# Two stages of an audio tower reordered: dispatch scores and the two-way scan

## The reference

```python
def _L1_attn_ref(x, ...):              # the two-way stage
    xn = layer_norm(x, ln_g, ln_b)
    xg, z = split(xn @ Wi + bi)
    f = simple_ssm(conv1d_same(xg, Wf_conv, bf_conv), af, bf, cf, df)
    bb = flip(simple_ssm(conv1d_same(flip(xg), Wb_conv, bb_conv), ab, bb, cb, db))
    zg = silu(z)
    return (f * zg + bb * zg) @ Wo + bo + x

# soft mixture; dispatch makes the logits, both softmaxes and the slots' inputs
    phi_n = phi * rsqrt(sum(square(phi), axis=0) + EPS_NORM)
    # logits of 374 tokens against 64 * 16 = 1024 slots;
    # softmax over tokens gives dispatch weights, softmax over slots combine weights;
    # slot inputs = dispatch weights^T @ tokens, then layer norm, 64 experts, combine
```

## Time and profile before

| what | value |
|---|---|
| median of 3 runs | 2442.38 us (2439.57 to 2445.49) |
| the profiled execution, its own time | 2446.13 us |
| its span in the trace | 2444.3 us |
| two-way stage in the trace | about 1698 to 1875 us |
| dispatch in the trace | about 1878 to 2201 us |
| mean granted clock of TensorE | 0.956 of full |

### The profile page before, as it was taken

The page is one execution under the profiler, slowest core; times in us unless marked ns, Lnnn a source line. Parts: engine busy times, 40 slices in busy tenths (PEclk is TensorE's granted clock), DMA queues, the critical chain, the costliest instruction groups (busy, mean ns, idle before and its releaser), DMA issues. The chain is left out here.

```text
span 2444.3 us, 45740 instructions
## 1 busy us (share of the span) xinstructions
PE 2208.8 (90%) x16643; PEld 2025.3 (83%) x16643; DVE 1361.5 (56%) x3616; ACT 1143.7 (47%) x2203; POOL 861.7 (35%) x760
## 2 busy tenths in 40 slices
PE   2999999999999999999999877976997888968988
PEld 1999999999999999999999876975554666658988
DVE  4676667667667667676666642413674555532222
ACT  1655655565555555555555532222442555532320
POOL 4444555555554554555655521102220000000000
PEclk9999999999999999999999987988998898988999
DMA  5700000000000000000000212492000011009966
GB/s 164 227 4 4 4 4 4 7 6 4 9 5 5 9 4 5 9 4 5 9 4 2 64 36 83 146 255 78 18 15 0 39 43 46 39 38 303 332 209 223
DMA packets 101337, 150.65 MB, mean 62 GB/s; under 512 B 14693, under 2 KB 79119, under 8 KB 100365
## 3 DMA queue, kind: packets, MB, share of 16 engines
q1 hardware_dynamic: 77580, 118.36, 15.4%
q10 hardware_dynamic: 17984, 20.30, 2.5%
q0 software_dynamic: 5568, 9.27, 1.3%
HBM read 102.32 MB, written 45.50 MB: 60 GB/s over the span
## 5 line engine op out<-in xcount | busy, mean ns | idle before, releaser
L290 PE MATMUL banks<-t_wt,t_l 128*128 128x128 f32 x8508 | 1045.9, 277 | 4.1 <-ACT t_l L367 2.9
L290 PEld LDWEIGHTS banks<-t_wt,t_l 128*128 128x128 f32 x8508 | 1015.5, 193 | 19.5 <-ACT t_l L367 4.1
L466 POOL TENSOR_TENSOR t_rstd<-t_var,t_minus_half 128x4 f32<-128x4 f32 (+1 forms) x379 | 367.0, 968 | 639.0 <-DVE t_var L395 637.6
L349 ACT ACTIVATE t_sq<-banks 128x512 f32<-128x512 f32 (+1 forms) x379 | 216.2, 570 | 523.1 <-PE banks L290 521.3
L403 DVE TENSOR_TENSOR t_yn<-banks,t_rstd 128x512 f32<-128x512 f32 (+1 forms) x379 | 249.0, 657 | 366.2 <-POOL t_rstd L466 364.4
L383 ACT ACTIVATE t_l<-banks,t_cols 128x512 f32<-128x512 f32 x376 | 286.8, 778 | 78.9 <-PE banks L339 76.2
L472 POOL TENSOR_TENSOR t_zrstd<-t_zvar,t_minus_half 128x8 f32<-128x8 f32 x188 | 307.6, 1637 | 25.4 <-DVE t_zvar L430 25.4
L392 DVE TENSOR_REDUCE t_ss<-t_sq 128x4 f32<-128x512 f32 (+1 forms) x379 | 244.5, 645 | 88.3 <-ACT t_sq L349 82.7
L367 ACT ACTIVATE t_l<-banks,t_cols 128x512 f32<-128x512 f32 (+1 forms) x381 | 285.1, 748 | 12.5 <-PE banks L299 7.7
L299 PE MATMUL banks<-t_ident,t_yn 128*128 128x128 f32 x1426 | 220.0, 274 | 13.0 <-DVE t_yn L403 11.7
L299 PEld LDWEIGHTS banks<-t_ident,t_yn 128*128 128x128 f32 x1426 | 173.3, 142 | 27.1 <-DVE t_yn L403 14.8
(11 more groups left out here) (324 smaller groups left out, 3332.5 us busy)
## 6 DMA issues: line engine op xcount, KB each, us to landing
t_w<-in_w SPq DMA_DIRECT2D x64, 480.0 KB
t_w<-in_w SPq DMA_DIRECT2D x27, 576.0 KB, 5.7
ect<-t_ECT SPq DMA_DIRECT2D x16, 750.0 KB, 3.2
t_l<-in_w1a SPq DMA_DIRECT2D x27, 384.0 KB, 4.3
sorted_by_expert<-t_h SPq DMA_DIRECT2D x4, 2400.0 KB, 11.0
routed_by_expert<-t_h SPq DMA_DIRECT2D x4, 2400.0 KB, 17.5
t_ectb<-ect ACTq DMA_DIRECT2D x5, 1500.0 KB, 7.9
t_w1x<-in_w1x SPq DMA_DIRECT2D x64, 97.5 KB
```

The source lines that it names most:

```text
L290: mm = pe.matmul(psY[bank][:, t * C:(t + 1) * C], src[:, at:at + P], T["wt"][:, 3 * (layer - 1) + k, :], start=(k == 0), stop=(k == 2))
L349: act.activation(T["sq"][:, par, 0:n], psY[bank][:, 0:n], ACT.Square).then_inc(S["squared"], 1)
L466: pool.tensor_tensor(T["rstd"][:, par, 0:n], T["var"][:, par, 0:n], T["minus_half"][:, 0:n], ALU.pow)\
```

## The change

In the two-way stage the transposes leave `inputs`: `turn(b + 1)` stands ahead of `conv(b, 2)`, and ACT's reads of them stand ahead of bu and du of m = 2. DVE runs `norm(b + 2)` ahead of batch b's scans and adds the output of batch b - 1 after batch b's two additions. The buffer u has three places instead of two, and both places of xh are used. The banks are dealt anew: the outputs get two banks of their own, and the third convolution shares the first one's. In dispatch the three tiles' logits stand in steps 3, 4 and 5 instead of 3 to 6, the turned logits have one bank instead of two, and the turned slot inputs get that second bank instead of sharing pE.

```diff
-    pA, pB, pX, pC, pO = ps[0], ps[1], [ps[2], ps[3]], [ps[4], ps[5], ps[6]], [ps[7], ps[1]]
+    pA, pB, pX, pC, pO = ps[0], ps[1], [ps[2], ps[3]], [ps[4], ps[5], ps[4]], [ps[6], ps[7]]
...
+            def turn(b):
+                pe.wait_ge(S["xh_ready"], b + 1)
+                turn_tiles(pe, T, xh, b, pA, pB).then_inc(S["xh_turned"], 1)
+
             def inputs(b):
-                pe.wait_ge(S["xh_ready"], b + 1)
-                if b >= 2:
-                    pe.wait_ge(S["two_out"], b - 1)
-                turn_tiles(pe, T, xh, 0, pA, pB).then_inc(S["xh_turned"], 1)
...
-                if b >= 1:
-                    pe.wait_ge(S["conv_read"], 6 * (b - 1) + 2 * (m + 1))
+                if m == 2:
+                    pe.wait_ge(S["conv_read"], 6 * b + 2)
+                elif b >= 1:
+                    pe.wait_ge(S["conv_read"], 6 * b - 2 * m)
...
+            turn(0)
+            for b in range(B):
                 inputs(b)
                 conv(b, 0)
                 conv(b, 1)
-                outputs(b - 1)
+                if b >= 1:
+                    outputs(b - 1)
+                if b + 1 < B:
+                    turn(b + 1)
                 conv(b, 2)
...
                 for m in range(3):
+                    if m == 2 and b + 1 < B:
+                        read_turned(b + 1)
...
             for b in range(B):
-                link = Link(dve, S["two_link"], 10, b)
+                if b + 2 < B:
+                    norm(b + 2)
+                link = Link(dve, S["two_link"], 9, b)
...
-                if b + 2 < B:
-                    norm(b + 2)
-                dve.wait_ge(S["two_done"], b + 1)
...
+                if b >= 1:
+                    add_out(b - 1)
+            add_out(B - 1)
...
-    LOGITS_AT, TILE_AT = {3: (0, 1), 4: (2,), 5: (3,), 6: (4, 5)}, {4: 0, 6: 1, 7: 2}
+    LOGITS_AT, TILE_AT = {3: (0, 1), 4: (2, 3), 5: (4, 5)}, {4: 0, 5: 1, 6: 2}
...
-    pT, pE, pC = [ps[4], ps[5]], ps[6], ps[7]
+    pT, pH, pE, pC = ps[4], ps[5], ps[6], ps[7]
...
-                if k >= 2:
-                    pe.wait_ge(S["edt_ready"], k - 1)
+                if k >= 1:
+                    pe.wait_ge(S["edt_ready"], k)
...
-                if pairs_before(at) >= 1:
-                    pe.wait_ge(S["ht_read"], 2 * pairs_before(at))
...
-                pe.wait_ge(S["ed_read"], chunks)
```

More of the change, by code:

```diff
@@ L1673, in _, with read_turned @@
             act.wait_ge(S["pads_zero"], 1)
-            for b in range(B):
+            def read_turned(b):
                 act.wait_ge(S["xh_turned"], b + 1)
@@ L1681, in _ @@
                                scale=T["lncol"][:, 1:2]).then_inc(S["n_ready"], 1)
+            read_turned(0)
+            for b in range(B):
                 if b >= 1:
@@ L1730, in norm, with add_out @@
                 norm_stats(dve, T, S, link, 2 * b, lambda t: htile(T, b, t), D)
-                at = lambda t: a[0:TOK, b % 2, t, :]
+                at = lambda t: a[0:TOK, b % 3, t, :]
                 link(norm_apply(dve, T, lambda t: htile(T, b, t), at))
                 norm_stats(dve, T, S, link, 2 * b + 1, at, D)
-                if b >= 1:
-                    dve.wait_ge(S["xh_turned"], b)
-                norm_apply(dve, T, at, lambda t: xh[0:TOK, 0, t, :]).then_inc(S["xh_ready"], 1)
+                if b >= 2:
+                    dve.wait_ge(S["xh_turned"], b - 1)
+                norm_apply(dve, T, at, lambda t: xh[0:TOK, b % 2, t, :]).then_inc(S["xh_ready"], 1)
+            def add_out(b):
+                dve.wait_ge(S["two_done"], b + 1)
+                for t in range(TPB):
+                    n = min(TOK, LEN - t * TOK)
+                    ins = dve.tensor_tensor(htile(T, b, t)[0:n], htile(T, b, t)[0:n],
+                                            pO[t // 2][0:n, (t % 2) * D:(t % 2 + 1) * D], ALU.add)
+                ins.then_inc(S["two_out"], 1)
             dve.wait_ge(S["sig"], 1)
@@ L1772, in _ @@
                 hb = T["h"][0:TOK, TPB * b:TPB * (b + 1), :]
-                link(dve.tensor_tensor(hb, hb, a[0:TOK, b % 2, :, :], ALU.add))
+                link(dve.tensor_tensor(hb, hb, a[0:TOK, b % 3, :, :], ALU.add))
                 link(dve.tensor_tensor(hb, hb, view(T["rows"][0:TOK, 2, :], [[0, TPB], [1, D]]), ALU.add))
-                if b + 2 < B:
-                    norm(b + 2)
-                dve.wait_ge(S["two_done"], b + 1)
[L1778 to L1783, removed]
+                if b >= 1:
+                    add_out(b - 1)
+            add_out(B - 1)
 def dispatch(nc, T, S, io):
@@ L1887, in slot_inputs, with slot_inputs_turned @@
                 mm.then_inc(S["xs_done"], 1)
-            def slot_inputs_turned(k, chunks):
+            def slot_inputs_turned(k):
                 p = k % PAIRS_B
@@ L1911, in _ @@
                 if k >= 2:
-                    slot_weights_turned(k - 2, k)
+                    slot_weights_turned(k - 2)
                 if k < STEPS:
@@ L1921, in _ @@
                 if pair_at(k) is not None:
-                    slot_inputs_turned(pair_at(k), k - 1)
+                    slot_inputs_turned(pair_at(k))
             for p in (2, 3):
@@ L1925, in _ @@
             for k in range(pairs_before(STEPS + 2), PAIRS_B * B):
-                slot_inputs_turned(k, STEPS)
+                slot_inputs_turned(k)
         @block.scalar
@@ L1952, in copy_slot_inputs @@
                     act.activation(view(T[name][:, :], [[P, 2 * P // SLOT], [1, SLOT]], 2 * p * (P // SLOT) * P + b * SLOT),
-                                   pE[0:r, at:at + 2 * P].rearrange("d (n s) -> d n s", s=SLOT), ACT.Copy)\
+                                   pH[0:r, at:at + 2 * P].rearrange("d (n s) -> d n s", s=SLOT), ACT.Copy)\
                         .then_inc(S["ht_read"], 1)
@@ L1975, in _ @@
                         act.wait_ge(S["ed_turned"], k - 2)
-                    act.activation(EDT[:, k % 3, 0:LEN], pT[k % 2][:, 0:LEN], ACT.Exp, bias=T["ltm"][:, k % 2:k % 2 + 1],
+                    act.activation(EDT[:, k % 3, 0:LEN], pT[:, 0:LEN], ACT.Exp, bias=T["ltm"][:, k % 2:k % 2 + 1],
                                    accum_out=T["zd"][:, k:k + 1]).then_inc(S["edt_ready"], 1)
@@ L2452, in s2 @@
                     sb(name, shape, dt, two)
-                s2("u", [TOK, 2, TPB, D])
+                s2("u", [TOK, 3, TPB, D])
                 s2("xh", [TOK, 2, TPB, D])
```

10 lines of the change are left out of this document (5 added, 5 removed).

## The result

The changed kernel takes 2408.84 us, the median of 4 runs (2408.14 to 2409.43); the kernel before takes 2442.14 us on the same chip, also 4 runs (2439.57 to 2445.49). The ratio is 0.9863, with a 95% interval from 0.9846 to 0.988. The range's bound of 2410 is inside the interval (2404.5 to 2412.8), but the forecast's own middle, 2420.5, is not.

A forecast was written before the change was run, and what follows sets the result against it. PE, the busiest engine but with gaps and below full clock, was taken to bound both stages; 6.5 us (two-way) plus 15.4 (dispatch) gave 21.9, from 2442.4 to 2420.5 us, range 2410 to 2432.

The forecast's parts named there:

- The two-way stage: Late start of 8.2 us, then rounds of 17.5 us instead of 19.34, last outputs waiting 2.6 us more: gain 6.5 us.
- Dispatch's term: Dispatch gains 15.4 us: six batches at 1.9 us (11.4) plus 4.0 us in the last batch.
- The step that failed: Dispatch, middle batches: 0.5 us taken off the 2.4 us gain for the clock falling at step 7's gaps, leaving 1.9.
- The term for the last batch's four steps: Dispatch, last batch: four steps save 0.95 us each (3.8), plus 0.2 at the first slot inputs; 4.0 us, between 2 and 6.
- the walk along the end of a batch: Dispatch, from fifth step: logits end after 8.82 us, next batch's first step 6.09 later, second 1.83 later; 2.4 us gained.
- 2.11 + 0.27: Dispatch, per batch at unchanged clock: logits end 2.11 us earlier, the two steps after them take 7.92 us instead of 8.19.
- (1): Dispatch keeps little: longer round trip or later ACT queue, a batch gains 0.5 us instead of 1.9; 2429 us, chance 0.16.
- (2): Two-way stage gains nothing: rounds cost 18.4 us and the 8.2 us late start eats the rest; 2427 us, chance 0.11.
- (3): Slower: dispatch's clock falls at step 7's gaps and stays down through the slot products; 2469 us, chance 0.06.
- (4): No difference: the stages' gains are handed back before the experts start; chance 0.05 with all near it.
- its last rival: Dispatch: by the skill's rule alone, the single bank with one more short gap a batch would speak for the lower bound.
- The named signs: Expected trace: y(0) near 1743, two-way rounds 17.5 us, batches 34.4 us apart, 16 us in last batch, L's wait gone or short.

The follow-up runs named there:

- e5: Changed kernel with POOL's gathers issued one batch earlier (batches 0 and 1 at the start): 2408.49 us, two-way stage 159.3 us.
- e6: e5 with the output addition of batch 6 moved, in the last batch, ahead of the third scans: 2405.1 us, two-way stage 156.4 us.
- e7: Changed kernel with 14 extra unused transposes on PE in step 7, ahead of the slot inputs: 2409.03 us, dispatch 300.4 us.
- e8: e2 with the same 14 unused transposes behind step 7's slot inputs in the old dispatch: 2425.82 us, dispatch 319.1 us.
- e3: e2 with the logits in steps 3, 4 and 5, banks dealt as before: 2432.08 us, dispatch 324.3 us.
- e2: New two-way stage with the dispatch of the kernel before: 2432.75 us, ratio 0.9966.
- e4: Changed kernel with the logits back in steps 3 to 6, new banks kept: 2418.45 us, dispatch 310.8 us.
- e1: New dispatch with the two-way stage of the kernel before: 2420.47 us, ratio 0.9913.
- e9: e7 with ACT's copy to H ahead of its reads of the tile in steps 6 and 7: 2412.54 us (one run).
- e11: e6 with the 14 extra transposes of e7 and the copy order of e9: 2401.22 us, ratio 0.9842.

## Why the prediction fell short

**The two-way stage was right step by step.** y(0) came 8.1 us late, measured from the stage's start (forecast 8.2), behind a wait of 6.21 us for batch 2's gather; e5 takes that wait away and brings y(0) back to 27.3 us. Rounds took 17.2 us up to y(5) (forecast 17.5). y(7) came 10.3 us earlier (forecast 9.1; the shorter rounds are where the difference comes from), and the last outputs waited 8.78 us (forecast 8.9), which e6 shortened by the 2.7 that the addition costs. Gain 7.6, forecast 6.5.

**Dispatch's term was mis-sized: 15.4 forecast, 23.6 measured.** Its parts, again from transposes of q to transposes of q:

| part of dispatch | before | after | gain | forecast |
|---|---|---|---|---|
| up to batch 0's transposes (starts 1879.0, 1866.3) | 25.7 | 24.9 | 0.9 | 0 |
| round of batch 0 | 35.1 | 35.2 | 0.0 | 0 |
| five rounds of 36.34 and 33.54 | 181.7 | 167.7 | 14.0 | 9.5 |
| last round, to the last batch's fourth step | 35.6 | 33.8 | 1.8 | 1.9 |
| from there to the last slot products | 20.3 | 15.0 | 5.3 | 4.0 |
| from there to the experts | 29.3 | 27.6 | 1.8 | 0 |

**The step that failed** is the one that reads "The changed order has gaps there too, of about 0.8 and 1.9 us in step 7. With the slot products now closer behind them, I take off 0.5 and use 1.9 us a batch." The gaps were there as named (0.57 and 1.79 us), and the clock fell behind them in four of the five rounds, but it cost less: the slow clock cost 0.79 us a round in place of 1.63. I had let the cost grow by 0.5 where it shrank by 0.84. That is 1.3 us a round, against which the gain at full clock was 1.96 instead of the 2.4 that I had worked out, and (1.3 - 0.4) x 5 = 4.5 us make up the difference of the third row. Why the cost of the clock shrank stays open; that it did, the rows show.

The last row is the clock as well: the last 48 slot products have the same shape and took 8.10 us after, at 1.00, and 9.78 before, at 0.83:

```profile
2142.88 8.10 PE L1895 MATMUL banks<-t_q,t_ED 125*128 125x192 f32 x48 [0.71 <-DVE t_ED L2075]
```

It comes with the banks: 8.1 us in all nine profiles with the new banks, 9.7 to 10.9 in the four with the old.

The term for the last batch's four steps was 1.3 us too small, in two places. The last four steps gave 4.5 us (11.33 to 6.80) where 3.8 was forecast: a step came to 1.7 us and not to the round trip of 1.85. The part ahead of them gave 0.75 (8.94 to 8.19) where 0.2 was forecast; the first slot inputs no longer wait 1.38 us for the shared bank. From one execution to another the piece varies: 15.0 to 16.0 us in the nine profiles with the new banks, and 20.3 or 22.4 in the four with the old.

The first row's 0.9 us is no gain of the order. The piece took 24.9 to 26.8 us in the nine profiles with the new banks and 23.6 to 25.7 in the four with the old, longer at the lower clock in each; at a like clock the new order is 1 us or more longer (26.8 at 0.69 against 25.7 at 0.70). The prediction had 0.6 of loss there. The kernel before was profiled in the longer kind and the changed kernel in a shorter one, which is luck.

**At full clock the walk along the end of a batch holds.** In e7 the fifth step is at 2027.85, the row behind the last logits at 2036.67, the next batch's first step at 2042.84 and its second at 2044.68; from its timeline, the wait behind the fill and the second step:

```profile
2042.29 0.30 PE L1907 MATMUL banks<-t_ident,t_xs 128*128 128x128 f32 x1 [0.30 <-ACT t_H L1965]
...
2044.68 0.54 PE L1866 MATMUL banks<-t_ident,t_L 125*128 125x125 f32 x3 [0.24 <-ACT t_EDT L1989]
```

That is 8.82, 6.17 and 1.84 us; the forecast had 8.82, 6.09 and 1.83. In e8, the old order at full clock, they are 10.92, 5.02 and 2.35, where the earlier trace rows have 10.93, 5.01 and 3.18:

```profile
2046.33 1.66 PE L1938 MATMUL banks<-t_ident,t_L 125*128 125x125 f32 x14
2048.18 0.54 PE L1866 MATMUL banks<-t_ident,t_L 125*128 125x125 f32 x3 [0.19 <-ACT t_L L1958]
...
2050.53 0.49 PE L1866 MATMUL banks<-t_ident,t_L 125*128 125x125 f32 x3
```

So the one wrong row in the forecast's sum was before's last piece: the 3.18 us from the first to the second step in the earlier trace rows held 0.83 us of slow clock (2.35 without it). I had counted it as order. (The first row is the fill.) Behind the second step another 0.5 us is gained up to the next transposes, which the forecast left out. Together 2.10 - 1.15 + 0.51 + 0.51 = 1.97 us, the 1.96 of the rounds.

**The split into scores and banks failed too.** "2.11 + 0.27" gave nearly all of the gain to the early scores. Alone they bring 1.0 us of dispatch, no more than noise, and at full clock their round is longer than the old one (35.34 against 34.71). The first share can only be had if ACT's later queue does not hold PE through a shared bank. The last batch's gain belongs to the banks alone, as forecast: from batch 7's transposes to the experts e3 takes 88.1 us and e2 87.2, e4 76.9 and after 76.4.

**The rivals.** (1) and (2) had too little gain; a batch gained 2.8, and the two-way rounds were 17.2. (3), the slower one, named the right lever, the clock at step 7's gaps, and turned out the other way round. (4) fell: every microsecond of the stages reached the experts. The Trainium skill (TensorE: Matmul & The Clock Gate, "A second HAM failure mode: psum-queue depth-cycling") says that short idles between groups, as a kernel cycles through banks, make the clock swing and cost throughput. That agrees with the unequal rounds here, which e7 and e8 make equal by filling the idle. What the prediction drew from it, that one bank fewer for the turned logits would make it worse, does not agree with the rows: the clock of dispatch rose from 0.87 to 0.91. The prediction calls this its last rival, but the list gives it no time and no chance of its own. Here the measurement decides, and the number of banks alone does not tell the clock.

**The named signs.** Of those that the prediction listed, the wait for nB, y(0), the rounds of the two-way stage, the last outputs and the wait for the exponential and for H in step 7 came as described. Batches were 33.5 us apart instead of 34.4, and 15.0 us passed in the last batch instead of 16. In the list of PE's waits for the five rounds after, none has a wait for L, which was 8.4 us before:

```profile
PE banks L1907 <- ACT t_H L1961: 9.0, 5, 1.8
PE banks L1866 <- ACT t_EDT L1985: 3.1, 6, 0.6
PE banks L1895 <- DVE t_ED L2075: 1.9, 4, 0.5
```

## What to carry to other kernels

When rows of one order are taken as durations for another, read the clock beside each: a piece of 3.18 us at the lower level was 2.35 us of order and 0.83 us of clock, and a forecast made from it counts the clock twice or with the wrong sign. Moving work earlier on one engine gained 1.0 us alone, which is within the noise, giving each of two chains a bank of its own gained 14.5, and both 21.2: look first for the bank, buffer or queue that two chains share, since it decides whether an earlier start is kept. Where an unchanged part varies by more than the effect, compare the lengths of the changed stages between events, in more than one execution where the code allows it, and ask the whole time only at the end.

## What the runs showed of the hardware

The granted clock fell behind gaps of 1.7 and 1.8 us in a stretch in which PE was otherwise busy: it was 0.86 to 0.95 in most rounds of dispatch, but not in all of them: behind the same gap of 1.8 us and with the same instructions, 8 of the 20 full rounds of after, e1, e5 and e6 kept 1.00. Fourteen more transposes in the gap, 1.66 us of them in e8, kept it at 1.00 in all 25 full rounds of the five kernels that have them, and shortened the old dispatch by 6.2 us (325.3 to 319.1) and the new one by 2.6 to 3.7 (303.0 and 304.1 to 300.4): in the stage's length, work that computes nothing paid for itself, though e7's whole time does not show it. Each kernel's rounds then had the same length within 0.01 us.

The fill cures the rounds only. In the last batch, which it does not reach, e8 took 22.4 us where the earlier trace rows have 20.27, and its sum of 6.2 us is that much smaller. And unchanged code of 1.7 ms took between 1697.7 and 1708.9 us from one profile to the next, which is more than most of the effects studied here. It is no difference between chips: e5 to e8 ran on one chip and span 1700.1 to 1708.9, e9 to e11 on another and span 1697.7 to 1708.4. The part from the experts on, unchanged too, took 236.7 to 240.9.
